# Second feed-forward of a fused kernel: gate and up projections as seven products of 2x2 parts in place of eight

## The reference

```python
x = x + jnp.tanh(g_xattn[0]) * _L0_xattn_ref(_layernorm(x, axis=-1), ctx_2048, ...)   # linear attention
x = x + jnp.tanh(g_ffn[0]) * _L0_ffn_ref(_layernorm(x, axis=-1), ...)                 # 512 -> 2048 gelu -> 512
x = x + jnp.tanh(g_xattn[1]) * _L1_xattn_ref(_layernorm(x, axis=-1), ctx_2048, ...)   # softmax over 64 rows
x = x + jnp.tanh(g_ffn[1]) * _L1_ffn_ref(_layernorm(x, axis=-1), ...)                 # experts
```

```python
logits = jnp.einsum('th,eh->te', x, gate_weight)        # 32 experts, softmax, the 8 largest kept
w_tg = jnp.einsum('tk,tkg->tg', top_val, onehot)        # a weight for each token and group
gu = gate_up_proj[dominant_experts]
dn = down_proj[dominant_experts]
h = jnp.einsum('th,goh->tgo', x, gu)
gate, up = jnp.split(h, 2, axis=-1)
act = jax.nn.silu(gate) * up
y = jnp.einsum('tgi,ghi->tgh', act, dn)
out = jnp.einsum('tg,tgh->th', w_tg, y)
```

## Time and profile before

| | |
|---|---|
| Median of 3 runs | 1870.97 us (1870.21 to 1871.59) |
| The profiled execution, its own time | 1873.45 us |
| Its span, first to last instruction | 1871.7 us |
| TensorE busy | 1831.1 us, 98% |
| VectorE busy | 995.4 us, 53% |
| ScalarE busy | 499.8 us, 27% |
| GpSimd busy | 318.6 us, 17% |
| HBM read and written | 94.78 and 32.64 MB |
| TensorE's mean granted clock | 0.996 of full speed |

### The profile page before, as it was taken

The page is one execution under the profiler, slowest core; times in us unless marked ns, Lnnn a source line. Parts: engine busy times, 40 slices in busy tenths (PEclk is TensorE's granted clock), DMA queues, the critical chain, the costliest instruction groups (busy, mean ns, idle before and its releaser), DMA issues.

```text
span 1871.7 us, 24531 instructions
## 1 busy us (share of the span) xinstructions
PE 1831.1 (98%) x9496; PEld 897.6 (48%) x9496; DVE 995.4 (53%) x2036; ACT 499.8 (27%) x745; POOL 318.6 (17%) x299
## 2 busy tenths in 40 slices
PE   8699999999999999999999999999999999999999
PEld 3445555544444444444444454544444444545444
DVE  5667777754555455553526453636455454546322
ACT  2324534311221221222112232222222222223211
POOL 1122322312012020202200011111111111111111
PEclk9989999999999999999999999999999999999999
DMA  4123443243323333240310200202020202010010
GB/s 159 51 65 123 140 130 102 91 131 78 102 69 105 109 79 107 68 109 1 90 51 12 86 31 18 82 18 77 20 75 12 88 12 82 18 46 24 18 51 29
DMA packets 145174, 129.01 MB, mean 69 GB/s; under 512 B 76642, under 2 KB 93154, under 8 KB 145058
## 3 DMA queue, kind: packets, MB, share of 16 engines
q1 hardware_dynamic: 145058, 127.45, 22.7%
HBM read 94.78 MB, written 32.64 MB: 68 GB/s over the span
## 4 chain that ended last, share of the span: by engine, by line
PE 83%; issue 7%; DVE 4%; DMA 2%; POOL 2%; ACT 1%; POOLq 0%; SPq 0%; DVEq 0%; ACTq 0%
PE bank L962 43%; PE bank L1051 17%; PE bank L1131 11%; PE bank L1031 4%; PE bank L971 3%; PE bank L1016 1%; PE bank L997 1%; POOL arena L936 1%; DMA arena<-x_after_ffn 1%; DVE arena L1317 1%; DVE arena L1384 1%; PE bank L1066 1%; PE bank L1093 1%; POOL arena L910 0%; DMA arena<-in_L_xattn_Wkv 0%
## 5 line engine op out<-in xcount | busy, mean ns | idle before, releaser
L962 PE MATMUL bank<-arena 128*128 128x512 f16 x4608 | 1044.4, 379 | 6.0 <-DVE arena L1338 3.9
L962 PEld LDWEIGHTS bank<-arena 128*128 128x128 f16 x4608 | 449.4, 98 | 526.4 <-DVE arena L1338 4.3
L1051 PE MATMUL bank<-arena 128*128 128x512 f16 x1536 | 352.1, 379 | 1.6 <-DVE arena L1545 1.6
L1131 PE MATMUL bank<-arena 128*128 128x512 f16 x1152 | 264.3, 379 | 0.9 <-POOL arena L936 0.9
L1051 PEld LDWEIGHTS bank<-arena 128*128 128x128 f16 x1536 | 150.0, 98 | 181.5 <-DVE arena L1545 2.1
L1230 ACT ACTIVATE arena<-bank,arena 128x512 f32<-128x512 f32 x128 | 99.5, 777 | 486.1 <-PE bank L962 482.6
L936 POOL TENSOR_TENSOR arena<-arena 128x512 f16<-128x512 f32 x96 | 111.0, 1156 | 671.7 <-ACT arena L1267 650.2
L1687 DVE SCALAR_TENSOR_TENSOR arena<-bank,arena 128x512 f32<-128x512 f32 x96 | 71.9, 749 | 273.9 <-PE bank L962 273.9
L1543 DVE TENSOR_SCALAR arena<-arena 128x512 f16<-128x512 f32 x128 | 73.5, 575 | 270.6 <-ACT arena L1230 270.6
L1131 PEld LDWEIGHTS bank<-arena 128*128 128x128 f16 x1152 | 112.6, 98 | 133.9 <-POOL arena L936 1.4
L1267 ACT ACTIVATE arena<-arena 128x512 f16<-128x512 f32 x96 | 60.4, 629 | 371.7 <-DVE arena L1699 371.7
(11 more groups left out here) (159 smaller groups left out, 1148.1 us busy)
## 6 DMA issues: line engine op xcount, KB each, us to landing
arena<-in_L_ffn_proj SPq DMA_DIRECT2D x64, 256.0 KB, 2.9
arena<-group_weights SPq DMA_DIRECT2D x64, 256.0 KB, 3.1
arena<-in_L_ffn_gate_up_proj SPq DMA_DIRECT2D x96, 96.0 KB, 2.0
x_after_attention<-arena SPq DMA_DIRECT2D x8, 1024.0 KB, 5.2
arena<-x_after_attention SPq DMA_DIRECT2D x8, 1024.0 KB, 5.5
x_after_ffn<-arena SPq DMA_DIRECT2D x8, 1024.0 KB, 4.3
arena<-x_after_ffn SPq DMA_DIRECT2D x8, 1024.0 KB, 7.5
arena<-in_x SPq DMA_DIRECT2D x7, 1024.0 KB, 5.5
```

What stands on the lines that cost most here:

```text
L962: m = e.matmul(bank[b][:, :], wT[l][:, c, tile * P:(tile + 1) * P], y[h][:, c, :], start=n == 0, stop=n == NPASS - 1)
L1051: m = e.matmul(bank[t][:, :], hv[h][:, 0, t * P:(t + 1) * P], w2T[l][:, j, :], start=j == 0 and i == 0, stop=j == NH - 1 and i == 2)
L1131: m = e.matmul(bank[t][:, :], hv[h][:, 0, t * P:(t + 1) * P], dnT[l][:, j, :], start=j == 0 and i == 0, stop=j == NR - 1 and i == 2)
```

## The change

The 128 gate rows and the 128 up rows of a tile are the two row parts of the weights, the features 0 to 255 and 256 to 511 the two column parts; the activations have the same two parts of features and two of tokens (`HT` = 256). This 2x2 by 2x2 product is made from seven products of parts (Strassen's algorithm in Winograd's form). Each product is 6 matmuls of 256 columns (three passes by two tiles of 128 features); a tile has 42 of them where it had 24 of 512.

- Seven forms of the weights (`F_A11` to `F_S1`), each in high and low part, take the place of gate and up weights: ScalarE scales and writes high parts (`fsplit`, `fhi`), GpSimd adds the forms and writes the low parts (`flo`, `flo2`). Five sixths of them are made in the first feed-forward; the last sixth (`pair_of_forms`) beside block 0 of the experts.
- The down weights now lie where the first feed-forward's weights were; they are loaded after its last `up` and split beside the first steps of the experts (`finish_weights`).
- The second norm's turned activations are copied twice on ScalarE (`mturn`); GpSimd subtracts, then makes four sums of 256 columns twice a block (`tsum`) and their low parts (`tlo`), ScalarE the high parts (`thi`).
- A tile is four groups on TensorE: `p16` (bank 4), `p45` (bank 5), `p7` (bank 4 again), `p23` (bank 6). Side tasks have bank 7 alone. Three matmuls of a token tile of `dn`, two tiles behind, stand after each group, and one side task after that.
- ScalarE copies product 1 (`p1_ok`); VectorE adds from the banks: one sum after `p16`, one after `p45`, two after `p7`, one after `p23`; silu then runs on SBUF, VectorE multiplies by up, GpSimd multiplies by the group weights (`mix`) and subtracts (`mhi`), ScalarE writes the high part between.
- The second layer's tasks are spread over 47 of a block's 48 places, the four reads apart from each other; beside the last block of the first feed-forward they go two at each place. `Y_SCALE` is halved.

```diff
+F_A11, F_A12, F_A22, F_S2, F_S3, F_S4, F_S1 = range(7)
+T_1, T_4, T_3, T_2 = range(4)
+HT = TOK // 2
+NQ = NR // 2
+Q_EARLY = 5
...
-          + [(how, n, t) for n in ("1", "2", "gate", "up", "d") for how in ("max", "col") for t in range(SIZE[n])]
+          + [(how, n, t) for n in ("1", "2") for how in ("max", "col") for t in range(SIZE[n])]
+          + [("max", n, t) for n in ("gate", "up", "d") for t in range(NR)]
+          + [("col", "s", t) for t in range(4 * Q_EARLY)]
           + [("both", "gw", 0)])
+N_D = len(GROUPS)
+
+GROUPS += ([("col", "d", t) for t in range(8)] + [("col", "s", t) for t in range(4 * Q_EARLY, 4 * NQ)]
+           + [("col", "d", t) for t in range(8, NR)])
...
+    def forms(w):
+
+        add("fsplit", w)
+        late.append(lambda: add("flo", w))
+        if GROUPS[w][2] % 2:
+            after(1, lambda: add("fhi", w))
+
+            def done():
+                add("flo2", w)
+                formed.update((w - 1, w))
+            after(2, done)
...
+        if ph == "L":
+            return [stats, *slow, norm(0), norm(1), turn(0, 2), *slow, turn(1, 3), *slow, turn(2), *slow, turn(3)]
+
+        def sums(p):
+            return [lambda: add("tsum", b, p), lambda: add("thi", b, p), lambda: add("tlo", b, p)]
+        return [stats, *slow, norm(0), norm(2), turn(0, 1), *slow, turn(2, 3), *slow, *sums(0), *slow,
+                turn(1), *slow, turn(3), *slow, sums(1)[0], lambda: add("router", b, banks=1), *sums(1)[1:]]
...
+    P_.ring, P_.turn = [7], 0
...
+        s0 = W_OF["s", 4 * Q_EARLY]
+        return ([split(t) for t in range(8)] + [last(7), loads(range(s0, s0 + 8)), None, None, None]
+                + [split(t) for t in range(8, NR)] + [last(NR - 1), None]
+                + pair_of_forms(s0) + pair_of_forms(s0 + 2))
...
-            add("ge", b, j, banks=1)
-            apart()
-            add("ue", b, j, banks=1)
-            apart()
-            for gg in range(j * P // INTER, ((j + 1) * P - 1) // INTER + 1):
-                if gg * INTER >= j * P and gg > 1:
-                    add("gload", b, gg)
-            add("mix", b, j)
...
+    for s in range(total + 2):
+        b, j = divmod(s, NR)
+        if s < total:
+            if j == 0 and b == 0:
+                finer = finish_weights()
+            if j == 0 and b + 1 < NB:
+                assert not side
+                side = attention_tasks(b + 1)
+        if 1 <= s <= total:
+            add("mix", s - 1)
+            if s + 1 < total:
+                due.append(s + 1)
+                group_load()
+        if s < total:
+            add("p16", s, at=4)
+        down(s - 2, (0,))
+        apart()
+        if s < total:
+            add("p45", s, at=5)
+        down(s - 2, (1,))
+        apart()
+        if 1 <= s <= total:
+            add("mhi", s - 1)
+        if s < total:
+            add("p7", s, at=4)
+        down(s - 2, (2,))
+        apart()
+        if s < total:
+            add("p23", s, at=6)
+            if j == 5 and 0 < b < NB - 2:
+                add("xload", "E", b + 2)
+        down(s - 2, (3,))
         apart()
...
+        def product(out, j, f, y, c0, col):
+
+            n = 0
+            for h, l in PASSES:
+                for c in range(2):
+                    m = e.matmul(out, forms_of[j // 2][l][:, c, f, (j % 2) * P:(j % 2 + 1) * P],
+                                 y[h][:, c0 + c, col:col + HT], start=n == 0, stop=n == 2 * len(PASSES) - 1)
+                    n += 1
+            return m
...
+            elif kind == "p16":
+                s = step[1]
+                b, j = divmod(s, NR)
                 y_ready(w, ("M", b))
-                project(step, gateT, j, yT[b % 2], ge_mm)
-            elif kind == "ue":
-                _, b, j = step
-                w.wait_ge(w_lo, n_lo["up"])
-                project(step, upT, j, yT[b % 2], ue_mm)
+                w.wait_ge(t_lo, 2 * (b + 1))
+                w.wait_ge(f_lo2, 2 * nth["flo2", W_OF["s", 4 * (j // 2) + 3]])
+                k = bank_free(step)
+                product(bank[k][:, 0:HT], j, F_A11, yT[b % 2], 0, 0)
+                product(bank[k][:, HT:TOK], j, F_S2, tT[b % 2], 2 * T_2, 0).then_inc(p16_mm)
+            elif kind == "p45":
+                s = step[1]
+                b, j = divmod(s, NR)
+                k = bank_free(step)
+                product(bank[k][:, 0:HT], j, F_A22, tT[b % 2], 2 * T_4, 0)
+                product(bank[k][:, HT:TOK], j, F_S1, tT[b % 2], 2 * T_1, 0).then_inc(p45_mm)
+            elif kind == "p7":
+                s = step[1]
+                b, j = divmod(s, NR)
+                k = bank_free(step)
+                product(bank[k][:, 0:HT], j, F_S3, tT[b % 2], 2 * T_3, 0).then_inc(p7_mm)
+            elif kind == "p23":
+                s = step[1]
+                b, j = divmod(s, NR)
+                k = bank_free(step)
+                product(bank[k][:, 0:HT], j, F_A12, yT[b % 2], 2, 0)
+                product(bank[k][:, HT:TOK], j, F_S4, yT[b % 2], 2, HT).then_inc(p23_mm)
...
+            elif kind == "flo":
+                k = step[1]
+                v, t = w_src(k), GROUPS[k][2]
+                w.wait_ge(f_hi, n)
+                if t % 2 == 0:
+                    e.tensor_tensor(form_dst(k, 1, F_A11, 1), v[:, 0:256].unsqueeze(1), form_dst(k, 0, F_A11, 1),
+                                    ALU.subtract).then_inc(f_lo)
+                else:
+                    u, k0 = w_src(k - 1), 4 * (nth["flo2", k] - 1)
+                    e.tensor_tensor(form_dst(k, 1, F_A12, 2), v.rearrange("p (f n) -> p f n", f=2),
+                                    form_dst(k, 0, F_A12, 2), ALU.subtract).then_inc(f_lo)
+                    w.wait_ge(f_lo, n)
+                    e.tensor_tensor(v[:, 256:512], u[:, 256:512], v[:, 256:512], ALU.add).then_inc(f_sum)
+                    w.wait_ge(f_sum, k0 + 1)
+                    e.tensor_tensor(u[:, 256:512], u[:, 0:256], u[:, 256:512], ALU.subtract).then_inc(f_sum)
+                    w.wait_ge(f_sum, k0 + 2)
+                    e.tensor_tensor(u[:, 0:256], v[:, 256:512], u[:, 0:256], ALU.subtract).then_inc(f_sum)
+                    w.wait_ge(f_sum, k0 + 3)
+                    e.tensor_tensor(v[:, 0:256], v[:, 0:256], u[:, 0:256], ALU.subtract).then_inc(f_sum)
+            elif kind == "flo2":
+                k = step[1]
+                w.wait_ge(f_hi2, 2 * n)
+                for v, f in ((w_src(k - 1), F_S2), (w_src(k), F_S4)):
+                    e.tensor_tensor(form_dst(k, 1, f, 2), v.rearrange("p (f n) -> p f n", f=2), form_dst(k, 0, f, 2),
+                                    ALU.subtract).then_inc(f_lo2)
...
+            elif kind == "p16":
+                s = step[1]
+                w.wait_ge(p1_ok, s + 1)
+                e.tensor_tensor(u_s[s % 2], bank[bank_of[step, 0]][:, HT:TOK], gate_s[s % 2][:, 0:HT], ALU.add).then_inc(c_ok)
+            elif kind == "p45":
+                s = step[1]
+                w.wait_ge(p45_mm, s + 1)
+                w.wait_ge(c_ok, c_nth(s, "p1"))
+                e.tensor_tensor(gate_s[s % 2][:, HT:TOK], bank[bank_of[step, 0]][:, HT:TOK], u_s[s % 2],
+                                ALU.add).then_inc(c_ok)
+            elif kind == "p7":
+                s = step[1]
+                w.wait_ge(p7_mm, s + 1)
+                e.tensor_tensor(u_s[s % 2], bank[bank_of[step, 0]][:, 0:HT], u_s[s % 2], ALU.add).then_inc(c_ok)
+                w.wait_ge(c_ok, c_nth(s, "p7"))
+                if s > 1:
+                    w.wait_ge(m_lo, s - 1)
+                e.tensor_tensor(prod_s[s % 2].rearrange("p (h n) -> p h n", h=2),
+                                bank[bank_of[("p45", s), 0]][:, :].rearrange("p (h n) -> p h n", h=2),
+                                u_s[s % 2].unsqueeze(1).to_broadcast([P, 2, HT]), ALU.add).then_inc(c_ok)
+            elif kind == "p23":
+                s = step[1]
+                w.wait_ge(p23_mm, s + 1)
+                w.wait_ge(c_ok, c_nth(s, "p5"))
+                e.tensor_tensor(gate_s[s % 2], bank[bank_of[step, 0]][:, :], gate_s[s % 2], ALU.add).then_inc(c_ok)
             elif kind == "mix":
+                s = step[1]
+                w.wait_ge(silu, s + 1)
+                w.wait_ge(scale_of["up"], 2)
+                w.wait_ge(c_ok, c_nth(s, "p45"))
+                e.scalar_tensor_tensor(out=prod_s[s % 2], in0=prod_s[s % 2], scalar=inv["up"], in1=gate_s[s % 2],
+                                       op0=ALU.mult, op1=ALU.mult).then_inc(prod)
```

498 lines of the change are left out of this document (331 added, 167 removed).

## The result

| | before | changed |
|---|---|---|
| median of four runs each | 1871.28 us | 1926.62 us (1924.11 to 1927.41) |
| ratio | | 1.0292, 95% interval 1.0274 to 1.031 |
| profiled execution | 1873.45 us, span 1871.7 | 1926.13 us, span 1924.3 |
| mean granted clock of TensorE | 0.996 | 0.980 |

The change makes the kernel slower by 2.9%. The forecast was 1883, range 1848 to 1908: the sign is right, the size is not, and the result lies outside the range.

What follows compares the result with a forecast made beforehand. TensorE's own work was taken as the bound. Saving 56.9 us against 43.0 of steady waits and 9.8, 8.8, 1.4, 2.6 and 3.0 gave +11.7 on 1873.45, 1885.2; less 2.5 for the median, 1883 us, range 1848 to 1908.

Steps and rivals of the forecast that it cites:

- What the seven products save: TensorE's gate and up products: 256-column matmuls at 109.2 ns each save 0.593 us a step, 56.9 us in all.
- Router chain: Blocks 1 to 7: VectorE's router work ahead of the seventh product's sum stalls TensorE 3.2 us, 7 times, 22.4 us.
- Softmax chain: Blocks 1 to 7: VectorE's softmax work ahead of silu's product and the next p16's sum stalls 2.0 us, 7 times, 14.0.
- The start: Experts' start: VectorE's queue through step 3's first sum, with statistics 7.5 us after the last down, adds 9.8 us.
- The late forms: Block 0, steps 4 to 7: weight forms on GpSimd delay two down matmuls by 4.5 and 4.3 us, +8.8; lower bound 0.
- Clock: TensorE at half clock after the longer new gaps, the start's and the forms' two, 1.7 us each: +3 us.
- Last block of the first feed-forward: Side tasks at twice the pace: scores behind the last turn (1.6), read behind the turned probabilities (1.0), +2.6 us.
- What the others must now do inside a step: Experts' steps: the engines' work fits but VectorE's order does not; long side tasks ahead of sums idle TensorE, 43.0 us.
- the rival of the lock: GpSimd locks VectorE out of shared SBUF ports: each chain +0.8 us, low halves +0.77 each; 1900 to 1912 us, chance 0.18.
- Faster with the waits hidden: Rival: half or more of the 43 us of steady waits hides, 1837 to 1862 us; chance 0.26.
- Dear matmuls of 256 columns: Rival: 256-column matmuls on TensorE cost 131.7 ns each, +91 on the forecast, 1974 us; chance 0.03.
- at nothing: Costs taken as zero: forms beside the feed-forward (69 us if uncovered), extra weight-load pieces; turned activations' subtraction on GpSimd counted elsewhere.

Runs made afterwards that it cites:

- The filled gap: Changed kernel with 60 TensorE multiplications of 128 columns of constants during the router chain's wait in seven blocks, the chain left whole: 1913.28 us.
- the last two: Router and softmax chains, feed-forward's last block, start and late forms all spread, both turns one place later: 1867.19 us; then the router put back one place: 1862.56 us.

## Why the prediction failed, by its own steps

What each term was and what the profile of the changed kernel shows in its place, in us:

| term of the sum | forecast | measured |
|---|---|---|
| What the seven products save | -56.9 | -56.9 (12 products in 1.31, 109.2 ns each) |
| Router chain | +22.4 | +30.4 (4.43 and six of 4.33) |
| Softmax chain | +14.0 | +11.7 (seven of 1.67) |
| Statistics and context split | +3.6 | +1.1 (six of 0.19) |
| GpSimd's sums | +3.0 | +2.9 (six of 0.48) |
| The start | +9.8 | +10.3 (11.26, 0.83, 0.53, 0.98, less the 3.29 of before) |
| The late forms | +8.8 | +9.2 (4.94, 3.28, 1.01) |
| The end | +1.4 | +1.5 |
| Clock, in the experts' part | +3 | about +19 (38 us of work at half the clock) |
| Last block of the first feed-forward | +2.6 | +18.6 (to the experts' start) |

The rows of the experts' part add up to 29, against the 34.2 by which it grew. The 5 us between are a term that the sum lacks: TensorE has 32 waits more there, and each costs 0.16 us beside its idle time, since the last matmul ahead of it is shown for 0.277 us where in a stream the next would start after 0.109. (The mean clock of 0.97 would give 25 us; but part of the half clock falls into the gaps themselves, where it costs nothing.)

**Right.** The saving, with its 109.2 ns. So was the decision against the Trainium skill, "TensorE: Matmul & The Clock Gate", section Back-to-back issue gap: by the estimate from its 81 ns at 128 columns, 256-column matmuls would have cost 25 ns more each, and no row shows that. The part *What the others must now do inside a step* holds in its mechanism and its places. Its total, 46.1 us for 43.0, is nearer than its parts: the router is 8.0 short, the softmax chain and the statistics 4.8 too much (by its own figures the statistics are 0.5 us a time, not 0.6). The start and the forms are right within half a microsecond, in part by luck: x was usable 10.1 us after the last down, not 7.5, because each issue took SyncE 0.9 us, which I had not priced, and VectorE was less backed up behind it than I had summed.

**The step that failed first: Clock, +3, where about 19 came.** I saw the half clock in the earlier trace rows and priced it for three gaps by the 3.4 us of the stretch after the first one. The router gaps, at 3.2 us, I left out of the sum, as shorter than the 3.65 us that had taken the clock down. They are 4.33 us and every one brings it, seven times. The filled gap shows the price, 2.2 us each, some 15 us; the other 4 fell at the start and behind the forms. The mechanism was on paper, inside a rival with chance 0.18 ("if the router gaps grow past 3.65 us"), and belonged into the sum. Two readings of it were wrong besides. There is no step at 3.65 us: in the changed kernel a wait of 2.08 us and one of 2.96 had the half clock behind them and one of 3.28 had not, so the router gaps might have brought it at 3.2 us as well. And 3.4 us was not the only length on record; the kernel before shows a longer one:
```profile
121.85 1.12 PE L971 MATMUL bank<-arena 128*128 128x128 f32 x4 [3.98 <-DVE arena L1330]
```
```profile
122.00:127.00 5.00, 5.00 (x14) 2.22 (x15) 2.44 (x7) 0.60 (x1) 0.00 (x0) 0.50 0.33 95
```

**Why 4.33 and not 3.2.** One operation of the chain took 1.52 us beside GpSimd's lower halves. That is 1.23 us more than alone, and 3.2 and 1.23 make 4.4. So the term was the bare chain, rightly sized, and what it lacked is the rival of the lock, which I had at 0.8 us a chain: right in kind. Shortening the rest of GpSimd's work took 0.36 us off the router gap; TensorE's waits for GpSimd went from 11.2 to 4.3 us over the whole run. No run takes the lower halves alone away.

**The second step that failed: Last block of the first feed-forward, +2.6, where 18.6 came.** I counted two neighbours (scores behind the turn, read behind the probabilities: 1.46 and 0.80 measured) and missed four: the first norms, whose turns come 2.8 us after the statistics begin where they had 5.5 (2.87 and 0.94), those of the second normalisation (2.08), and the router behind GpSimd's lower half of the turned activations (2.96), which stands on GpSimd since this change. I had checked only that TensorE had nothing to wait for there before. And these gaps too brought the half clock, 6.4 of the 18.6 us; spread out, the same block runs at 1.00. With the waits, 10.0 us more than before, and 2.0 us ahead of the block that is the 18.6. (Some 3 us of it are this execution's luck with the clock, as the four other starts of the experts show.)

**The rivals.** Faster with the waits hidden: wrong, none was. The lock: nearest to what came, but its 1900 to 1912 still lacks the feed-forward's end. Dear matmuls of 256 columns: wrong, by the 109.2 ns. The point *at nothing* nearly holds: beside the forms there are three waits of TensorE's for VectorE between 808 and 856 us that were not there before (1.43, 0.44, 0.15), 2.0 us up to the last block; that the forms are their cause no run shows.

## What to carry to other kernels

Price a wait of TensorE together with what stands behind it: here a gap of 4.3 us cost 6.5. Where your sum gives gaps of 2 to 4 us, put both outcomes of the clock into the range, since here such gaps came out either way, and try filling the gap before anything else. When an engine that runs in order gets more short tasks that must be on time, look at the longest piece ahead of each of them, cut it, and put every reader one place behind its writer; then look again, since the wait often moves to the next reader. A change that loses 2.9% as written won 0.5% when only the order around it was mended.

## What the runs showed of the hardware

- After each of seven gaps of 4.3 us TensorE ran at half its clock, for 5.6 to 5.8 us in three and 3.3 to 3.6 us in four; in the three the fall came inside the gap, in the four at its end. The gaps of 1.7 us in the steady blocks brought none. Between these it went either way: 2.08 and 2.96 us brought it in the changed kernel and 3.28 us did not, and the same 2.96 us brought none in the run with GpSimd made short. 60 matmuls of constants in the gap (3.5 us, 1.0 us of idle left) kept the clock at 1.00. The Trainium skill, "TensorE: Matmul & The Clock Gate", section HAM oscillation — how this bites in real kernels, describes a kernel that pays for the clock again behind every wait of its tiles; this trace agrees, with 2.2 us on the mean behind the router gaps.
- Over the experts' first 110 us the mean clock was 0.89 to 0.94 in nine kernels, and no higher where 9 us of waits were gone but gaps of 4 us were left. In the last two, with no gap over 3.6 us there, it was 0.97 and 0.95.
- SyncE took about 0.9 us for each issue of down weights (eleven in 10.1 us, for eight tiles). The load behind them went out that much later, though the queue had stood idle before.
- A small VectorE operation on two SBUF inputs (128x128, 0.29 and 0.37 us alone) took 1.22 to 1.88 us when it met a GpSimd instruction of 1.16 to 2.12 us, and ended 0.15 us after it in the four cases read. Moved by one place, both were short again, and the block fell from 98.11 to 97.05 us.
